# Two-layer attention kernel: the first layer's softmax shift in a spare row of the third score product, and four gating units ahead of their splits

## The reference, cut to what matters

```
xn = layernorm(x)                      # each row of xn sums to zero
# attention of layer 0
k, q, v = xn @ Wk.T, xn @ Wq.T, xn @ Wv.T
e = q @ (k @ Wa.T).T                   # 1024 x 1024 scores
s = softmax(e) @ (v @ Wb.T)
# MLP of layer 0, hidden width 512, ternary weights
h = silu(lin(xn, w1)) * lin(xn, w2)
h = gelu(lin(h, h1)); h = gelu(lin(h, h2))
x = x + s * silu(lin(h, w3))
# layer 1: a gated 8-head recurrence plus a 16-head softmax attention
# and a mixture of 8 experts (top 2), combined in the same way
...
```

## Time and profile before

| | us |
|---|---|
| median of 3 runs | 1000.63 (1000.05 to 1000.78) |
| the profiled execution, own time | 999.73 |
| its span, first to last instruction | 997.9 |
| TensorE busy | 953.5 (96%) |
| ScalarE busy | 742.0 (74%) |
| VectorE busy | 551.2 (55%) |
| GpSimd busy | 195.0 (20%) |
| mean granted TensorE clock | 0.992 |

### The profile page before, as it was taken

The page is one execution under the profiler, slowest core; times in us unless marked ns, Lnnn a source line. Parts: engine busy times, 40 slices in busy tenths (PEclk is TensorE's granted clock), DMA queues, the critical chain, the costliest instruction groups (busy, mean ns, idle before and its releaser), DMA issues.

```text
span 997.9 us, 20056 instructions
## 1 busy us (share of the span) xinstructions
PE 953.5 (96%) x8050; PEld 538.2 (54%) x8050; DVE 551.2 (55%) x1342; ACT 742.0 (74%) x915; POOL 195.0 (20%) x142
## 2 busy tenths in 40 slices
PE   4999999999899999999989999999999999999996
PEld 3788643343388863334358884334436887433431
DVE  6655735645456654564565574456447467356354
ACT  5543699989763379998956449999895436999886
POOL 1200202522210020340230002134122003024122
PEclk9899999999999999999999999999999999999998
DMA  6000133000000023200000012310000001320000
GB/s 252 1 1 1 21 48 67 1 3 2 1 22 1 1 36 49 51 2 2 2 22 1 0 14 40 50 34 1 2 1 22 1 1 20 48 46 2 2 2 24
DMA packets 17649, 22.31 MB, mean 22 GB/s; under 512 B 2992, under 2 KB 14352, under 8 KB 17296
## 3 DMA queue, kind: packets, MB, share of 16 engines
q1 hardware_dynamic: 17552, 20.99, 10.4%
HBM read 7.85 MB, written 2.10 MB: 10 GB/s over the span
## 4 chain that ended last, share of the span: by engine, by line
PE 75%; ACT 10%; DVE 8%; issue 6%; POOL 1%; DMA 0%; DVEq 0%; ACTq 0%; POOLq 0%
PE ps L1135 74%; ACT big L1086 6%; DVE st L280 1%; ACT xn L1058 1%; DVE wk L747 1%; ACT spl L1039 1%; DVE wk L571 1%; DVE mx L492 1%; PE ps L1155 1%; POOL st L898 1%; DVE xn L460 0%; DVE spl L468 0%; ACT qz L1034 0%; DVE flags L428 0%; DMA xnext<-in_x 0%
## 5 line engine op out<-in xcount | busy, mean ns | idle before, releaser
L1086 ACT ACTIVATE big<-ps 128x1024 f32<-128x1024 f32 x512 | 491.0, 1042 | 35.9 <-PE ps L1135 35.4
L1135 PE MATMUL ps<-big,vaug 128*32 128x512 f32 x2048 | 272.6, 604 | 3.8 <-DVE wk L747 2.3
L1135 PE MATMUL ps<-hid 32*128 32x512 f32 x1024 | 130.6, 492 | 5.8 <-ACT big L1086 4.0
L1135 PE MATMUL ps<-hid,fw_sb 128*128 128x512 f32 x416 | 101.2, 397 | 0.3 <-DVE hid L476 0.3
L1002 ACT ACTIVATE wk<-ps,cols_sb 128x512 f32<-128x512 f32 x64 | 40.5, 687 | 80.2 <-PE ps L1135 74.4
L898 POOL TENSOR_TENSOR st<-st 128x4 f32<-128x4 f32 x16 | 16.2, 1010 | 388.1 <-DVE st L560 288.0
L1135 PEld LDWEIGHTS ps<-hid 32*128 32x128 f32 x1024 | 49.3, 181 | 78.8 <-issue 43.0
L912 POOL TENSOR_TENSOR qz<-qz,wk 128x512 f32<-128x512 f32 x32 | 41.2, 1287 | 237.8 <-DVE wk L717 237.8
L1135 PEld LDWEIGHTS ps<-hid,fw_sb 128*128 128x128 f32 x416 | 77.5, 188 | 18.5 <-DVE hid L476 1.1
L1135 PEld LDWEIGHTS ps<-big,vaug 128*32 128x32 f32 x2048 | 41.1, 108 | 70.1 <-issue 36.5
L735 DVE SCALAR_TENSOR_TENSOR big<-ps,sm,big 128x128 f32<-128x128 f32 x128 | 44.2, 345 | 46.7 <-PE ps L1135 36.0
(11 more groups left out here) (221 smaller groups left out, 1577.2 us busy)
## 6 DMA issues: line engine op xcount, KB each, us to landing
hid<-spl SPq DMA_DIRECT2D x288, 32.0 KB
xnext<-in_x SPq DMA_DIRECT2D x4, 512.0 KB, 4.0
big<-in_fw SPq DMA_DIRECT2D x1, 1877.0 KB, 8.8
out<-qz SPq DMA_DIRECT2D x7, 256.0 KB, 2.3
hid<-one_row SPq DMA_DIRECT2D x16, 96.0 KB
wk<-in_lw SPq DMA_DIRECT2D x1, 1476.0 KB, 13.7
big<-in_fw SPq DMA_DIRECT2D x1, 939.0 KB, 10.7
cst_sb<-in_cst SPq DMA_DIRECT2D x1, 440.0 KB, 4.4
```

Source lines behind the costliest of these rows:

```text
L1086: up(ms_exp, a.activation(prob[:, at:at + 2 * CH].rearrange("p (h n) -> p h n", n=CH), ps[:, bank:bank + 2, :], ACT.Exp, scale=HDM ** -0.5))
L1135: return t_.matmul(out_, lhsT, rhs, start=start, stop=stop, **kw)
```

## The change

Four edits. First, G is replaced by G less its last column: from each row of G its last element is subtracted, and since each row of xn sums to zero the scores stay what they were, while the last row (127) of `r` becomes exactly zero in both parts. Second, that spare row of `spl[:, 1, :]` takes `negrow`, and the operand it is multiplied by becomes `x_one` (= `spl[:, 2, :]`): rows 0 to 126 a copy of `xt_hi`, row 127 ones. One product now gives high-by-low and the shift, so a score unit has three products and not four. Third, `x_one` is filled by three transfers per sequence on SyncE (127 rows by 512 columns twice, and the row of ones), and the zeroing on GpSimd goes. Fourth, in the first half of the MLP VectorE gates a unit before it splits the previous one.

```diff
-        negrow, shift = spl[0:1, 2, :], spl[:, 2, :]
+        negrow, x_one = spl[P - 1:P, 1, :], spl[:, 2, :]
...
+            sp.wait_ge(x_lo.sem, 2)
             sp.wait_ge(wide_ok, 1)
...
+            def key_rows(c):
+                sl = slice(c * CH, (c + 1) * CH)
+                return sp.dma_start(x_one[0:P - 1, sl].bitcast(F32), xt_hi[0:P - 1, sl].bitcast(F32))
+
+            def ones_in_last_row():
+                return sp.dma_start(x_one[P - 1:P, :].rearrange("p (a n) -> p a n", n=P).bitcast(F32),
+                                    one_row[0:1, :].bitcast(F32).unsqueeze(1).broadcast_to([1, S // P, P]))
+
+            for c in range(NCH):
+                up(x_one_in, key_rows(c), 16)
+            up(x_one_in, ones_in_last_row(), 16)
             for b in range(B):
...
-                sp.wait_ge(shift_zero.sem, shift_zero.at(b, 0))
                 sp.wait_ge(neg_ok.sem, neg_ok.at(b, 1))
...
                     up(x_in, load_x(b + 1), 16)
+                    for c in range(NCH):
+                        sp.wait_ge(x_hi.sem, x_hi.at(b, 3 + c))
+                        up(x_one_in, key_rows(c), 16)
+                    up(x_one_in, ones_in_last_row(), 16)
...
-            done(v.tensor_copy(xn[:, 5 * D:6 * D], ps[:, 0, 0:D]), "Wa Wk")
+            done(v.tensor_copy(mrow[:, :], ps[:, 0, D - 1:D]))
+            so_far()
+            done(v.tensor_scalar(xn[:, 5 * D:6 * D], ps[:, 0, 0:D], mrow[:, 0:1], None, ALU.subtract), "Wa Wk")
...
-                for m in range(KM):
-                    gate_unit(0, m)
+                gate_unit(0, 0)
+                gate_unit(0, 1)
+                gate_split(0, 0)
+                gate_unit(0, 2)
+                gate_split(0, 1)
+                gate_unit(0, 3)
+                gate_split(0, 2)
+                gate_split(0, 3)
...
-                up(shift_zero, g_.memset(shift.bitcast(I32), 0))
...
-                    split3(ps[:, SC_BANKS[n_], :], *tok(jt), spl[:, 0, sl], spl[:, 1, sl], True, False)
+                    with_high(ps[:, SC_BANKS[n_], :], *tok(jt), spl[:, 0, sl])
...
+                t_.wait_ge(x_one_in.sem, x_one_in.at(b, 48))
                 t_.wait_ge(negrow_in.sem, negrow_in.at(b, 16))
...
-                    up(sc_mm, mm(ps[:, SC_BANKS[n_], :], one_row[:, :], shift[:, h * CH:(h + 1) * CH], False, True))
+                    up(sc_mm, mm(ps[:, SC_BANKS[n_], :], x_one[:, jt * P:(jt + 1) * P], spl[:, 1, h * CH:(h + 1) * CH], False, True))
```

More of the change, by code:

```diff
@@ L225, in build_program @@
         maxT, neg_ok, negrow_in = sig("maxT"), sig("neg_ok"), sig("negrow_in", 16)
-        shift_zero = sig("shift_zero", 1, 1)
+        x_one_in = sig("x_one_in", 48)
         l1_mm, l1_act, hid_hi, hid_lo = sig("l1_mm", 16), sig("l1_act", 8), sig("hid_hi", 24), sig("hid_lo", 24)
@@ L485, in gate_unit, with gate_split @@
                     up(gated, v.scalar_tensor_tensor(h_, ps[:, L1_BANKS[c][m % 2] + 1, :], col("w2s", m), h_, ALU.mult, ALU.mult))
+                def gate_split(c, m):
+                    n_ = c * KM + m
                     v.wait_ge(gated.sem, gated.at(b, n_ + 1))
@@ L551, in _ @@
                     gate_unit(1, m)
+                    gate_split(1, m)
                 act_units(0, 8, 1)
@@ L883, in _ @@
             g_.memset(half, -0.5).then_inc(half_set, 1)
-            g_.memset(shift.bitcast(I32), 0).then_inc(shift_zero.sem, 1)
             g_.wait_ge(half_set, 1)
@@ L1308, in _ @@
                         score_products(n_)
-                    h = n_ // NT
+                    h, jt = n_ // NT, n_ % NT
                     if b == 0 and n_ == 13:
```

## The result

The changed kernel takes 1005.33 us, the median of seven runs (1004.76 to 1009.14), against 1000.61 us for seven runs of the kernel before: a ratio of 1.0053, with an interval of 1.0042 to 1.0064. It is slower. The forecast was 1003.0 us, slower, in a range of 987 to 1042. The profiled execution took 1006.0 us, its span 1004.1 us at a mean granted clock of 0.990. One run of all that are told of here, one of the five of the kernel with 112 and 15 rows, took 1266.94 us at a granted clock of 0.664; its ratio leaves that run out, and nothing here explains it.

The account below looks back on a forecast made before the run. TensorE was taken to bound the kernel, with 75% of the chain. 999.73 + 7.9 (first sequence) - 5.5 (other three) = 1002.1 us for the profiled execution, 1003.0 on the median's scale; range 987 to 1042.

Parts of the forecast that it names:

- a hole's clock: TensorE after the first sequence's 9 us wait: clock falls to 0.5, costing 0 to half of 9 us, taken as 2.
- the limits that the prediction had set itself: Prediction falls if a copy takes under 9.5 or over 12.5 us, or the hole's clock costs more than 4 us.
- The idle time before the transpose: Sign in the profile after: transpose released by VectorE's last maximum, TensorE idle about 0.45 us before it.
- One engine: Each 127-row copy into `x_one` goes over one DMA engine, 127 being prime; chance 0.52 near the loads' pace, 0.20 slower.
- The pace: `x_one` copies on one engine: 24.9 GB/s as in the opening loads, 10.45 us a copy.
- The pace of the earlier trace, 26.8 us a copy: Rival for the `x_one` copies: SBUF-to-SBUF pace of 9.7 GB/s, 1134 us in all; one engine, slower, had chance 0.20.
- The first sequence: TensorE waits for the copies until 50.2 us: +8.7, less 2.78 for units 4 to 15, plus 2 for clock: +7.9.
- The other sequences: Later three sequences: TensorE goes on at 285.9, not 284.96, +0.94 less 2.78: -1.84 us each, -5.5 in all.
- The edits priced at nothing: VectorE's two setup instructions for G, GpSimd's dropped memset and the new gating order: 0 us of their own.
- the hidden case: Rival: copies spread over 16 engines land in time, all four sequences gain 12.6 us, 988.0 us; chance 0.23.
- ScalarE's distance of 0.516 us: Score stage, units 12 to 15: exponentials follow each other by 0.516 us without a gap, costing 0.1 us once.
- that rival: Score stage turns to ScalarE: exponentials keep 0.60 us, 0.7 us more a sequence, 991 if copies hidden; no separate chance.

Follow-up runs that it names:

- 112 and 15 rows: Changed kernel with each 127-row copy made as two transfers, of 112 and of 15 rows: 986.53 us, ratio 0.9851.
- 113 rows: Changed kernel with each 127-row copy made as two transfers, of 113 and of 14 rows: 996.79 us, ratio 0.9955.

## Why the prediction was right, point by point

The mechanism and the direction held: one engine carries a copy, TensorE waits for it, and the wait outweighs the products removed. The size was too small: +2.4 us were forecast and +4.7 measured on the medians. On the profiled execution, 1002.1 us forecast and 1006.0 measured, 3.8 of the 3.9 us missing are 1.75 in the first sequence, 0.97 in the other three and 1.10 in the start. The waits were mis-sized, and the start had no term. That the forecast on the median's scale is only 2.3 us off is scatter: the profiled execution of before was a short one and that of now a long one. A copy at 10.7 us and a hole's clock at 2.4 lie inside the limits that the prediction had set itself. The idle time before the transpose, 0.18 us in the profile where 0.45 was forecast, was the sign that came out otherwise.

**One engine.** Right. The step was read across from 16 completions for 128 rows and 8 for 8, without a row that showed an odd number; 254 packets with two completions, and the runs with 112 and with 113 rows, show it. The Trainium skill's rule (DMA: Bandwidth & Descriptors, "Why a DMA increments its semaphore by 16 and not by 1"), the largest divisor up to 16 of the slowest dimension, gave the same, and the runs agree with it: 127 and 113 rows on one engine, and 112, 15 and 14 rows with 16, 15 and 14 completions.

**The pace.** Right: 10.45 us a copy from the loads at the start. Both copies took from about 30.9 to 52.3 us, 10.7 each, with a slow beginning of 8 to 22 GB/s, then 25 to 27 GB/s. The pace of the earlier trace rows, 26.8 us a copy, comes from copies on eight engines and doesn't hold for one; why they are slower no run here shows. The Trainium skill's figure for one engine (same page, "Specifications"), about 27 GiB/s, is 29 GB/s; the trace shows less here too.

**The first sequence.** The direction and cause were right, the size too small: +7.9 forecast, +9.65 measured. The mis-sized term is the wait, 10.85 us for 9.2, and in it the two ends of the transfers more than their pace. I had the first copy issued 0.56 us after `wide_ok`; it was 0.9 (28.64 to 29.54). I had the copies at full pace from the first packet; their first 2.6 us of data ran at 8 to 22 GB/s, and both together took 0.5 us longer than forecast. And I had TensorE go on 0.1 us after the last data; it was 0.8 (52.3 to 53.08). The clock, taken as 2 between 0 and 4.5, was 2.4. Ahead of the wait, from the transpose to the third products, the 112 and 15 kernel gains 0.33 us (3.44 to 3.11), where the sum had 0.51.

**The other sequences.** -1.84 each forecast, -1.23, -1.87 and -1.45 measured. The products removed gave what was said, but TensorE stood for 2.1 us, not for 1.45 (0.94 and the 0.51 gained ahead). From the end of `xt_hi`'s first half to TensorE's going on it was 297.51 - 272.65 = 24.9 us, forecast as 24.1. The order on that engine (copies, shares of the stores, maxima's row) was right: the run with the stores later took 1.4 us a sequence off it. They weigh 1.4, not the 1.8 of their data.

**The start.** +1.10 us, for which the sum had nothing. The load of the tokens landed after 4.59 us in this profile and 3.92 in that of before, 0.67, which no edit touches. The rest opens at the second pair of products with `spl`: it starts 0.66 us later than before (21.90 against 21.24), and the product behind it 1.12 later (22.89 against 21.77), since two products take 0.99 us there and took 0.53. With G's edit alone the same 0.99 us stand there, the first transpose is at 38.8, not 38.05, and the median doesn't move.

**The edits priced at nothing.** G's edit and the gating order are worth 0 on the kernel before, as said. For the hidden case the prediction said 988.0 us, and 112 and 15 rows gave 986.5: 3.4 to 4.0 us a sequence, not 3.16 (steps between transposes of 239.8, 237.4 and 237.1 us against 243.5, 240.8 and 241.0). 3.26 of it lies between the transpose and the end of the scores (2.91 of that in units 4 to 15, for which the sum had 2.78); the remainder lies elsewhere in the sequence and stays open. ScalarE's distance of 0.516 us was right as 0.512, and with it that rival fell.

**What was left out.** The hold of the third transfer's issue. I had SyncE free behind it, and it was held for 10.11 us; "short", as I called an issue on SyncE above, is wrong for it. It costs little. In the later sequences the stores wait for their data until 5.7 us ahead of the transpose anyway (5.75 in the earlier trace rows, 5.63 with the row of ones first), and went out 4.91 ahead: the hold delayed them by some 0.8 us. With the row of ones first it didn't delay them at all, and the wait was longer. In the first sequence that run settles less: the maxima's row left SyncE at 44.19 us there and at 45.24 in the changed kernel, so it was held in both; but TensorE needs the copies as well, and their data move until 52.3.

## What to carry to other kernels

Before a tile's edge row is given another use, count what the remaining rows divide into: from the earlier trace rows and two completions one sees that 127 rows, or 113, go over one engine at 25 GB/s, while 112 and 15 go over 16 and 15 and take an eighth of the time, for one more issue of about 1 us. Splitting each copy in two turned 0.5% slower into 1.5% faster here, so when a change takes real work away and the time rises, look for the one new wait before giving the change up. And price a hole in TensorE's work by more than its length: the products behind it may run at half the clock.

## What the runs showed that I had not expected

SyncE takes 0.66 us to issue the row of ones behind copies on 16 engines, and 10.11 us behind two copies on one engine, in the first sequence as in the second. With the row of ones first, the maxima's row was held for 4.94 us (first sequence), and the two stores, which came later, hardly (3.74 us against 2.98 in the earlier trace rows). An issue can thus wait for transfers on the way, though no semaphore says so. In the four such holds that I counted, the end did not depend on which issue was held: it came when 154 or 155 of the 254 rows had moved, at 44.35 and 287.32 us in the changed kernel, at 44.19 us with the row of ones first, and at 286.95 us (second sequence) with the stores later. What sets that number stays open.

Of three holes of one length, 2.63 us idle, one (the third sequence's) was followed by the clock's fall, which cost 1.6 us, and the others were not. Holes of 1.98 us brought none in the changed kernel's profile. Two of its seven runs took 1008.5 and 1009.1 us, with mean clocks of 0.987 and 0.986 against 0.990 in the profiled one; they would fit further falls of this kind, but have no profile to show it.

The clock row can mislead near the start. From 23 to 28 us the products of 128 by 128 stand 0.21 us apart in the changed kernel, as they do in the stretch of 0.50 of the kernel before, and in the second sequence 0.11 us apart; yet the row says 1.00 for both of the changed kernel's stretches. Before its first fall a 1.00 is thus no proof of full speed. The distance between starts is. And a mean clock some thousandths lower can come from this stretch alone: 0.992 in the profile of before and 0.997 in that with only G's edit, whose span is 0.9 us longer.

The same gating order is worth nothing on one kernel and 3.7 us on the other. An edit measured alone says little about what it is worth beside the one it was made for.
